# ScalarE copies every second pair of cross scores into SBUF, VectorE takes those maxima there, and the merged order is drawn anew

## The reference

```
q2 = _heads(xq @ ed_wq)
wei2 = jnp.einsum('bhtd,bhjd->bhtj', q2, k2) * scale
wei2 = jax.nn.softmax(wei2, axis=-1)
ed_out = _merge(jnp.einsum('bhtj,bhjd->bhtd', wei2, v2)) @ ed_wproj + ed_bproj
```

## Time and profile before

| | |
|---|---|
| median of 3 runs | 364.31 us (364.25 to 364.96) |
| the profiled execution | 364.14 us |
| its span in the trace | 362.4 us |
| granted TensorE clock over the span | 0.999 |

### The profile page before, as it was taken

How to read it: one execution, slowest core, us unless ns; L and a number is a source line. 1 busy time by engine, 2 the same in 40 slices (tenths; PEclk the granted TensorE clock), 3 DMA queues, 4 the chain that set the end, 5 groups by cost and what they waited for, 6 DMA issues and landing times.

```text
span 362.4 us, 9692 instructions
## 1 busy us (share of the span) xinstructions
PE 345.5 (95%) x4142; PEld 263.0 (73%) x4142; DVE 228.0 (63%) x563; ACT 170.9 (47%) x299; POOL 52.7 (15%) x67
## 2 busy tenths in 40 slices
PE   8889999998999999999999999999999999999995
PEld 5657788977766778766766878776887767686473
DVE  5799897636498657749867555839924384452611
ACT  3277652462852455643661474651652725403442
POOL 2033421050320010140200040510200211000000
PEclk9999999999999999999999999999999999999999
DMA  7986121000100003100000030000000000000000
GB/s 200 257 317 263 29 71 43 0 2 2 27 2 2 0 3 87 29 13 14 5 2 0 4 87 2 2 14 13 3 0 2 4 2 13 3 2 15 2 2 25
DMA packets 5397, 14.13 MB, mean 39 GB/s; under 512 B 785, under 2 KB 3078, under 8 KB 5098
## 3 DMA queue, kind: packets, MB, share of 16 engines
q1 hardware_dynamic: 5210, 13.43, 12.2%
q10 hardware_dynamic: 144, 0.08, 0.1%
HBM read 12.59 MB, written 0.92 MB: 37 GB/s over the span
## 4 chain that ended last, share of the span: by engine, by line
PE 82%; DVE 11%; ACT 4%; issue 2%; ACTq 0%
PE ring L504 39%; PE ring L746 8%; PE acc L650 7%; PE ring L625 5%; PE ring L760 5%; PE ring L605 4%; DVE negmax L1034 4%; PE ring L599 3%; PE ring L637 3%; DVE negmax L1013 2%; PE ring L669 2%; ACT exps L859 2%; PE ring L711 1%; PE ring L536 1%; PE ring L617 1%
## 5 line engine op out<-in xcount | busy, mean ns | idle before, releaser
L1034 DVE TENSOR_REDUCE negmax<-ring 112x2 f32<-112x750 f32 x64 | 56.9, 935 | 19.3 <-PE ring L746 18.8
L859 ACT ACTIVATE exps<-ring 125x896 f32<-125x896 f32 x48 | 41.4, 915 | 47.3 <-PE ring L760 46.9
L1247 POOL TENSOR_SCALAR_AFFINE_SELECT exps<-exps 112x896 f32<-112x896 f32 x32 | 31.3, 1004 | 112.9 <-ACT exps L859 112.9
L1013 DVE TENSOR_REDUCE negmax<-ring 112x8 f32<-112x896 f32 x32 | 33.4, 1085 | 22.1 <-PE ring L605 22.0
L650 PE MATMUL acc<-exps,v 125*17 125x112 f32 (+1 forms) x1280 | 38.9, 261 | 0.2
L746 PE MATMUL ring<-k,q 32*112 32x376 f32 x256 | 37.8, 518 | 1.3 <-DVE negmax L1034 0.5
L650 PEld LDWEIGHTS acc<-exps,v 125*17 125x17 f32 (+1 forms) x1280 | 28.1, 97 | 12.8 <-issue 10.0
L859 ACT ACTIVATE exps<-ring,pad 112x896 f32<-112x896 f32 x32 | 30.5, 1006 | 10.2 <-PE ring L637 10.1
L504 PE MATMUL ring<-w_b,h 128*112 128x256 f32 x128 | 29.3, 382 | 0.0
L504 PE MATMUL ring<-n,w_b 128*128 128x224 f32 x128 | 26.1, 358 | 0.9 <-DVE negmax L1013 0.7
L504 PEld LDWEIGHTS ring<-w_b,h 128*112 128x112 f32 x128 | 22.1, 177 | 5.5 <-issue 0.9
(11 more groups left out here) (139 smaller groups left out, 548.1 us busy)
## 6 DMA issues: line engine op xcount, KB each, us to landing
c_nat<-in_ctx SPq DMA_DIRECT2D x4, 672.0 KB
w_b<-in_w_b SPq DMA_DIRECT2D x1, 2304.0 KB, 12.4
xk_t<-in_xk_t SPq DMA_DIRECT2D x8, 224.0 KB, 5.4
w_a<-in_w_a SPq DMA_DIRECT2D x1, 1280.0 KB, 6.0
xh<-in_keys SPq DMA_DIRECT2D x4, 224.0 KB, 3.5
x_nat<-in_x SPq DMA_DIRECT2D x4, 224.0 KB, 3.9
out<-x SPq DMA_DIRECT2D x8, 112.0 KB, 1.9
rows_sb<-in_row SPq DMA_DIRECT2D x1, 560.0 KB, 7.7
```

What stands on the lines that cost most here:

```text
L859: return nc.scalar.activation(exps[0:k, EXP_AT[job], :, :], o[0:k, :, 0:4 * T], ACT.Exp, bias=bias)
L1013: v_max[b].step(nc.vector.tensor_reduce(negmax[0][:, slot(g, b), 2 * m_:2 * m_ + 2, :], o[0:T, :, 0:4 * T].rearrange("p r (j t) -> p r j t ...
L1034: x_max[b].step(nc.vector.tensor_reduce(negmax[1][:, b, 2 * m_:2 * m_ + 2, i], o[0:T, :, 0:S], AX.X, ALU.max, negate=True), g, 2 * i + m_ + 1)
L1247: p_masked[b].step(nc.gpsimd.affine_select(e, e, [[0, 8], [1, T]], ALU.is_ge, 0.0, base=0, channel_multiplier=-1), g, k)
```

## The change

In each `cS` step the first pair of banks is read by DVE as before. The second pair is copied by ACT, as one instruction of 112x750, into one of NCS = 3 new SBUF tiles `cs_sb`, which `COPY_AT` deals out in turn. PE may refill the second pair when the copy is done. DVE waits for the copy and reduces from the tile. ACT waits, before it overwrites a tile, for the reduction that read it three copies earlier (`COPIED_BEFORE`). `MIX` is another string with the same letters. An argument of the program's builder, `dynamic_dma_scratch_size=1024`, makes room in SBUF for the new tiles; the program issues its DMAs from SP and ACT.

```
+NCS = 3
-MIX = ("AALNNLCANDEEDCDNPIWDNDWCPJEWJIDPCCJPDICJNCPJIAPAJRAAIPCIHDJIHEPECDECPEDCJDCDIAHJIPAAJKANIAABIBJBIJPABEFCAFPBNFBEBBFPBBFC"
+MIX = ("NAALNLDENCAEDCNDPIDNWDWCPJEWIJDPCCIDPJCNPPJICJIAIPRAJAIHCHCJAEDPCEDPEDCJDCDIAHIJPAIAKANJAPAEBPFIFABPBPDJIJFEBHBNEBAEFPBB"
...
+SCORES = [step for step in ORDER if step[0] == "cS"]
+COPY_AT = {step: i % NCS for i, step in enumerate(SCORES)}
+COPIED_BEFORE = {step: SCORES[i] for i, step in enumerate(SCORES[NCS:])}
...
+        cs_sb = [sb(f"cs_sb{i}", [T, 2, S]) for i in range(NCS)]
+        c_s = each("cross_scores_copied", 4)
...
-"cS": lambda: (x_max[i[0]], 2 * i[1] + i[2] + 1),
+"cS": lambda: (c_s[i[0]], i[1] + 1) if i[2] else (x_max[i[0]], 2 * i[1] + 1),
...
+            def cross_scores(g, b, i):
+                step = ("cS", g, b, i)
+                o = is_filled(act, step + (1,))
+                if step in COPIED_BEFORE:
+                    _, g_old, b_old, i_old = COPIED_BEFORE[step]
+                    act.wait_ge(*x_max[b_old].at(g_old, 2 * i_old + 2))
+                c_s[b].step(nc.scalar.activation(cs_sb[COPY_AT[step]][:, :, :], o[0:T, :, 0:S], ACT.Copy), g, i + 1)
...
             def cross_maxima(g, b, i):
-                for m_ in range(2):
-                    o = is_filled(dve, ("cS", g, b, i, m_))
-                    x_max[b].step(nc.vector.tensor_reduce(negmax[1][:, b, 2 * m_:2 * m_ + 2, i], o[0:T, :, 0:S], AX.X, ALU.max, negate=True), g, 2 * i + m_ + 1)
+                o = is_filled(dve, ("cS", g, b, i, 0))
+                x_max[b].step(nc.vector.tensor_reduce(negmax[1][:, b, 0:2, i], o[0:T, :, 0:S], AX.X, ALU.max, negate=True), g, 2 * i + 1)
+                dve.wait_ge(*c_s[b].at(g, i + 1))
+                x_max[b].step(nc.vector.tensor_reduce(negmax[1][:, b, 2:4, i], cs_sb[COPY_AT["cS", g, b, i]][:, :, :], AX.X, ALU.max, negate=True), g, 2 * i + 2)
...
-    nc = bacc.Bacc("TRN2", target_bir_lowering=False, num_devices=1)
+    nc = bacc.Bacc("TRN2", target_bir_lowering=False, num_devices=1, dynamic_dma_scratch_size=1024)
```

More of the change, by code:

```diff
@@ L117 @@
            "R": [("rows",)], "L": [("flag",), ("general",)]}
-MIX = ("AALNNLCANDEEDCDNPIWDNDWCPJEWJIDPCCJPDICJNCPJIAPAJRAAIPCIHDJIHEPECDECPEDCJDCDIAHJIPAAJKANIAABIBJBIJPABEFCAFPBNFBEBBFPBBFC"
-       "PFBFEPNDPBEFFBDECNFDFPBBFKFPBNFBDBCFDCPHEBDEBCPBCDBFAEFAJAFCADPBBDFCPDBCNPFCIDCBDPFFAJIFAJFIFABPAKFBPAKFBIBFBJBIJPHHBIPB"
-       "JIJKEPBEEFIHJBBBIJPIBJEFIFIBJFJBPFBEFEFEPEFEFFBBFBFKFBHBFFBKBFFFBBBFBFKBFFFBFFFBFF")
+MIX = ("NAALNLDENCAEDCNDPIDNWDWCPJEWIJDPCCIDPJCNPPJICJIAIPRAJAIHCHCJAEDPCEDPEDCJDCDIAHIJPAIAKANJAPAEBPFIFABPBPDJIJFEBHBNEBAEFPBB"
+       "BBDFECBFPBEFFFPCNFNBDPBNFNBKFBPDFBFBKDCEBDPFCFPCBDCCEBBBFAJAAFPCBDPBCJFDCADCFPCBFDFDFFAPPIAFJHAABKFAFIBBBEFBPBJJIHBPJFII"
+       "BIKBJIFEFBFEEBJBIHIJEIBJFIPJIJBEFEFEFFFEBPEFBFBKFBPBBHBFFPBFFKBFBBBFBFKBFFFFBFFBFF")
 def merged():
@@ L370, in filled_and_taken @@
                     "h": lambda: (a_h, 4 * i[0] + 4), "cT": lambda: (v_ct, i[0] + 1), "k2": lambda: (a_k2, C * (i[0] + 1)), "shift": lambda: (a_shift, 2),
-                    "v2": lambda: (v_v2, i[0] + 1), "cS": lambda: (x_max[i[0]], 2 * i[1] + i[2] + 1),
+                    "v2": lambda: (v_v2, i[0] + 1), "cS": lambda: (c_s[i[0]], i[1] + 1) if i[2] else (x_max[i[0]], 2 * i[1] + 1),
                     "cM": lambda: (c_m[i[0]], 1), "cX": lambda: (c_exp[i[0]], 2 * i[1] + i[2] + 1),
@@ L934, in _ @@
                  "t1": out1_transposed, "xqT": normed2, "q2": query2, "h": hidden, "cnorm": context_normed, "cT": context_hi, "k2": key2, "split": weights_hi, "shift": shifts_copied,
-                 "cM": cross_max_rows, "cX": cross_exp, "cO": cross_out, "t2": out2_transposed})
+                 "cS": cross_scores, "cM": cross_max_rows, "cX": cross_exp, "cO": cross_out, "t2": out2_transposed})
         @block.vector
```

## The result

The changed kernel takes 368.05 us (median of 5, 367.74 to 368.55) against 364.42 us for the kernel before in the same session: a ratio of 1.0099, 95% interval 1.0074 to 1.0124. It is 3.6 us slower. 360.9 was forecast, with a range up to 365.6, so the time lies on the other side of no change and outside the range.

A forecast was written before the change was run, and what follows sets the result against it. PE was taken as the bound, with gain only from its waits behind maxima of cross scores. Profiled 364.14 - 7.5 + 0.9 + 3.2 = 360.7 us, on the median 360.9 (-0.9%), range 356.5 to 365.6.

The forecast's parts named there:

- The copies' own cost: 32 added ACT copies of 112x750 at 798 ns each, 25.5 us in all, lying beside PE.
- the +0.9 us for ACT's queue: PE's 6.0 us of waits for ACT grow in step with ACT's load, 15%: +0.9 us, from 0 to 6.4.
- The SBUF reductions: 32 DVE reductions change only their source to SBUF; 0.4 us less and off the path, taken as 0.
- The order: New MIX brings V and O steps closer together, so PE waits for ACT's copy of the sums; +3.2 us, from 0.
- the relief: Two thirds of PE's waits behind maxima of cross scores vanish; 7.5 us, from 3.7 to 11.2.
- The prediction's last sentence: Said the redraw was priced by the few places standing closer together, not by the many that moved a little.
- the start that was left at 0: At the program's start q0 of group 1 moves up and waits between 0 and 1.1 us; taken as 0.
- the pool: PE's waits behind maxima of cross scores: 9.6 us in the cross-score group plus 1.6 at other products, 11.2 us.
- the 10.3 us: Excess of the cross-score group's 39.1 us over 28.8 us for 32 undisturbed cS steps at 0.90 us each.
- the sign laid down in the prediction: Cross-score group falling to about 31 us busy would show it right; staying above 35 us means the second rival.
- the second rival: DVE's rate stays the bound at first pairs of cross scores; a third of the pool relieved, 364.7 us; chance 0.14.
- The third rival: ACT becomes late, copies standing among exponentials that PE waits for; 367.3 us at eight such copies; chance 0.16.

The follow-up runs named there:

- e11: Kernel before with the new MIX, plus at each cS place an unneeded SBUF-to-SBUF ACT copy of 112x750 that waits for no scores; 371.2 us, 1.019.
- e4: Changed kernel with DVE's reduction of the copied pair cut to 8 of 375 columns; 367.88 us, 1.0099 to the kernel before.
- e6: Kernel before, MIX unmoved, with the copies of second pairs, and ACT's copy of the sums moved from the O step to the V step; 369.3 us, 1.0162.
- e2: Kernel before with the copies, in the old order with three cross-score steps moved by one place; 384.25 us, 1.0558.
- e8: Changed kernel with ACT's copy of the sums at V and three places of MIX spread again between V and O; 369.48 us, 1.0159 to the kernel before.
- e12: As e6, but ACT copies the second pair in only five of the 32 cS steps; 364.41 us, 1.0003 to the kernel before.
- the new head with the old tail: Kernel before, no copies, with the changed kernel's order up to position 241 of 322 and its own order behind; 372.48 us, 1.022.
- e1: Kernel before with only the new MIX, no copies, both pairs reduced from PSUM; 371.48 us, 1.0195.
- e3: Kernel before with only the three moves of cross-score steps that e2 has, no copies; 369.96 us, 1.0143.
- e9: Changed kernel, but DVE reduces a copied pair behind the next step's first pair, the last one ahead of cM; 374.59 us, 1.0278 to the kernel before.
- e10: As e6, but DVE reduces a copied pair behind the next step's first pair, the last one ahead of cM; 367.79 us, 1.0092 to the kernel before.
- e13: Kernel before, no copies, with its own order up to position 241 of 322 and the changed kernel's order behind; 366.45 us, 1.0059.

## Why the prediction was wrong

**The copies' own cost: right.** 25.5 us on ACT, 797 ns each. ACT's load as such is free in the new order (e11), so the +0.9 us for ACT's queue measured as nothing. **The SBUF reductions: right** at no gain: 934 against 937 ns. The fixed parts in the Trainium skill ("VectorE: DVE Perf Modes", the errata of SBUF-src ops) would have made a difference of 65 ns, an estimate from that page; the trace doesn't agree, it shows 3.

**Two terms of the sum failed.** The order was 3.9 us too cheap and the relief 4.1 us too large; less the 0.9 that didn't come, that is the 7.1 us between forecast and measurement. With the measured terms the sum is 364.3 + 7.1 - 3.4 = 368.0 us.

**The new order was priced at 3.2 us and costs 7.1.** The places that were priced are `O` and `V` steps, and these two kinds cost 3.2 + 0.8 = 4.0 us, near the 3.2. That is in part luck: the two waits of 0.76 us and the one at `V 1 0 0` came as priced, the three of 0.30 were 0.17 or 0.18, and one of 0.59 us at `O 2 1 1` had not been priced. What was left out is the rest of the redraw, +1.9 at self scores and +1.3 at cross scores above all (e11 against before). Why self scores wait longer in it was not followed step by step. The prediction's last sentence named this danger and gave it no price in the sum. Two starts show where it builds up. PE has done the same steps in both orders when it begins `v1 1` in the old one and `X 0 1 1` in the new one, and again when the first `cX` of group 3 begins. Timeline of PE, before, then e11, then the changed kernel:

```profile
75.23 0.47 PE L504 MATMUL ring<-w_a,n 128*112 128x256 f32 x1
...
328.04 0.37 PE L625 MATMUL ring<-maxrows,sel 32*125 32x224 f32 x2
```

```profile
75.84 0.47 PE L628 MATMUL ring<-maxrows,sel 32*112 32x224 f32 x8
...
336.05 0.37 PE L628 MATMUL ring<-maxrows,sel 32*125 32x224 f32 x4
```

```profile
75.97 0.36 PE L634 MATMUL ring<-maxrows,sel 32*112 32x224 f32 x4
...
332.94 0.37 PE L634 MATMUL ring<-maxrows,sel 32*125 32x224 f32 x4
```

By 75 us e11 is 0.6 behind, by 328 us 8.0; the last 30 us give 0.9 back. Everything up to the first mark, the start that was left at 0 included, costs 0.6 us. Between the same marks the copies save 336.05 - 332.94 = 3.1 us, and 3.24 counted from 75 us.

**The relief was taken as 7.5 us and is 3.2 to 3.4.** The mechanism is real. The largest places are three of about 0.7 us and two of 0.4. One of them, `cS 2 0 3` in e11, and the same in the changed kernel:

```profile
252.61 1.64 PE L749 MATMUL ring<-k,q 32*112 32x376 f32 x8 [0.33 <-DVE negmax L1046]
```

```profile
250.44 0.90 PE L755 MATMUL ring<-k,q 32*112 32x376 f32 x8 [0.33 <-DVE negmax L1050]
```

The hole for the second pair is gone, and the 0.33 us for the first pair stays, as forecast. What was wrong is the pool: all of the excess over 0.90 us a step was put down to DVE's maxima. In the changed kernel 38.5 - 28.8 = 9.7 us of excess remain, and e4 shows that the reductions from SBUF have no part in it. Three steps (`cS 1 1 2`, `3 1 1`, `3 1 3`) take 1.9 to 2.1 us instead of 0.90. The first of them, timeline of the changed kernel:

```profile
190.48 0.81 PE L755 MATMUL ring<-k,q 32*112 32x376 f32 x4
...
190.69 1.73 ACT L876 ACTIVATE exps<-ring 125x896 f32<-125x896 f32 x2 [0.43 <-PE ring L769]
...
191.66 0.89 PE L755 MATMUL ring<-k,q 32*112 32x376 f32 x4 [0.37 <-ACT exps L876]
```

The bank of the second pair is held by scores of a `cX` whose exponential ACT takes first. A copy of cross scores doesn't free it. In the earlier trace rows this very wait stands with 0.39 us; the prediction took its idle time off and left the longer hole inside the step in the pool. The trace of the kernel before tells how much of the 10.3 us was of which kind. A pair's first weight load (rows of PEld) starts about 0.04 us behind the release of the pair where it waited for it (0.1 us where PE had run empty), so each step's excess can be put down to what it waited for last. Counted like this, 4.6 us end with a reduction of cross scores, 3.5 with ACT (exponentials 1.7), 2.1 with other work of DVE, and 0.1 are left. Only 2.0 of the 4.6 us are in steps that waited last for a former second pair, the kind that a copy frees. With the 1.6 us at other products the pool was some 6.2 us and not 11.2, and the prediction then counted two thirds of the larger one as relieved. In the changed kernel the same count gives 3.4 us behind reductions of first pairs, 5.9 behind ACT and 0.8 behind others (10.1 in all and not 9.7, since two steps that overlap are counted apart).

**Which rival.** By the sign laid down in the prediction, a group above 35 us busy (35.9), the second rival came closest, and its relief of 3.7 is near the 3.4 measured. Its forecast of 364.7 us was still over 3 us too low, and its reason isn't the cause: DVE's rate is refuted by e4, though waits for single first pairs remain. The third rival, a late ScalarE, didn't happen in the changed kernel (the chain's ACT share is 5%, and PE waits for `acc_sb` and exponentials no longer than in e11, where nobody waits for the copies), but it is what happens without the redraw: 5.0 us in e6, and 19.9 with e2's moves against before, the lower clock in them included. So copies and redraw belong together: of the orders tried, only in the new one do all 32 copies gain. It costs 7.1 us, and they return 3.4 of it. That every order that suits the copies must cost so much isn't shown. The Trainium skill ("VectorE: DVE Perf Modes", "Rules for kernel authors") advises a copy to SBUF only where many operations follow. Here one follows. The runs agree with the advice in the old order, where the copies lose 5.0 us, and not in the new one, where they give 3.4. What decides in these runs is whether ACT reaches the copy in time, since PE and DVE both wait for it.

**What stays open.** Whether another order exists that carries the copies for less than 3.4 us. e8 tried three small edits of the order and was no better; nothing was searched. Whether copies at only those steps whose second pair PE waits for would gain in the old order, which e12 was meant to show. Why the new head with the old tail is the worst of the four was not followed.

## What to carry to other kernels

A stage moved to an engine that is half idle costs nothing by its load and much by its place: ask what stands ahead of it in that engine's queue, and which engine then waits behind it in turn. When a change carries a redrawn order with it, run the order without the change before believing a price made of its visible places; here they were little more than half of it. Count as relieved by an edit only holes whose releaser is the one that the edit makes earlier, and look inside a step for it, not only at the idle time ahead of it. The step that gains is the one that takes the bank next, so choose the steps to change by who held the bank.

## What the runs showed of the hardware

Neither the kernel before nor the changed one shows a granted clock below full in the middle of its profiled execution. The profiled executions of e1, e2, e3, e6, e9, e10 and e13 do. Windows of e1 (columns: window, length, busy of PE, PEld, DVE, ACT, POOL, granted clock, DMA share, GB/s):

```profile
120.90:124.30 3.40, 2.71 (x21) 1.12 (x14) 3.14 (x6) 0.54 (x1) 0.00 (x0) 1.00 0.03 7
124.30:127.70 3.40, 3.40 (x10) 3.08 (x11) 1.36 (x4) 0.00 (x0) 0.00 (x0) 0.50 0.00 0
127.70:131.10 3.40, 3.40 (x21) 2.82 (x19) 0.29 (x3) 1.71 (x5) 0.00 (x0) 1.00 0.00 0
```

A stretch at 0.50, the 1.2 GHz of the two levels, follows one in which PE was busy for 2.71 of 3.40 us. It costs about 1.7 us: the 16 matmuls of `h 1 1` that it falls on took 4.98 us, and 3.29 in e11, which has the same order and no such stretch. The profiled execution of e1 took 372.94 us, its three others 371.20 to 371.53, which is where e11 lies (371.09 to 371.56). So a difference of one or two us between single profiled executions can be such a stretch alone, and e11 was the trace to compare. Medians can hold it too. In e9 the stretch from 181.06 to 184.47 us has 0.50, behind 3.46 us in which PE was busy for 1.39, and all four executions show a mean clock of 0.994 or 0.995. e10 took 369.41 us with a stretch (0.993) and 367.54 to 367.82 in the three executions at 0.998 or 0.999. So a change that makes PE wait longer in one place can, as in e9, also bring such a stretch, and its price is then more than the wait.
